# Eight weight products of a selected-token network: four of them moved from the rounds of a selection into the making of a list

## The chip, the cores and the metric

The kernel runs on one core of one Trainium2 chip. The metric is the device time in microseconds (us) of one execution. The median of three runs of the kernel before is 1208.15 us (1207.38 to 1210.46). A change smaller than 0.3% of that, 3.6 us, is called no change in this document.

## The reference, cut to what matters

The whole computation is a graph network, a linear-attention mix and, last, a feed-forward network on about half of the nodes. Only the last part is touched:

```python
# _L0_ffn_ref, x: (1, 6250, 256), the layer-normed output of what comes before
weights = (einsum('bsd,do->bso', x, wr) + br)[..., 0]      # one weight a node
_, idx = top_k(weights, k)                                 # k = 3125
sel_idx = idx[:, :kk]                                      # kk = 3124 nodes
sel = take_along_axis(x, sel_idx[:, :, None], axis=1)
h = gelu(einsum('bkd,dh->bkh', sel, w1) + b1)              # 256 -> 1024
y = einsum('bkh,hd->bkd', h, w2) + b2                      # 1024 -> 256
y = y * weights of the selected nodes
out = zeros.at[sel_idx].set(y) + x
```

## The kernel before

The five engines run five separate programs, each in the order in which its code is written. They wait for each other through semaphores. That written order is what sets the order of the work here; there is no scheduler.

Nodes are handled in tiles of 128, and four tiles make a group. The node stage (13 groups) ends near 994 us of the trace. From there the kernel does this:

- **The rounds of the selection.** The threshold of the top 3124 weights is found digit by digit: nine counts. In each, VectorE compares (L1256), counts (L1258) and raises `s_c`; TensorE sums the counts over the partitions with one small matmul into `psN` (L2087) and raises `s_n`; VectorE reads the sums. After the last round come two matmuls on `marks` (L2092, L2093), some VectorE work, and two transposes (L2096, L2097).
- **The blocks of the list.** The 3124 indices are made in `LBLOCKS` = 7 blocks of 512. For block b, VectorE makes `step_` ("reached", L1309); TensorE multiplies it ("ranks", L2105, into `psR` or `psC` in turn); VectorE compares into `below` ("ranked", L1316); TensorE counts with eight matmuls of one column ("places", L2112 and L2113, into `psI`, which is `psKx[1]`); VectorE writes the indices ("listed", L1320). TensorE issues `ranks(b + 1)` ahead of `places(b)`. GpSimd gathers the chosen rows `yg` by the list (L464). After the places of blocks 2, 3, 4 and 5 TensorE also transposes tile 0, 1, 2 and 3 of the first group of chosen rows (L2125, into `psT`). ScalarE copies each to `yT_hi` (`y_high`, L1751), and VectorE makes `yT_lo` (`y_low`, L1303). `y_low` of tile t stands in VectorE's program behind "ranked" of block t + 3 and ahead of "reached" of block t + 5.
- **The last network.** For each group of chosen rows the first layer (`hidden`, by L56 to L58, into `psG` = `psQ + psKx`), Gelu on ScalarE (L1763), and the second layer (L65 to L68).

All float32 weights are split into a high part (rounded to the fast matmul type) and a low part. The low part is the raw weight minus the high part, and TensorE computes it: `low_product(i)` is one float32 matmul by the identity (L2081) and one by minus the identity on the high part (L2082), each 128x512. ScalarE copies each product out of PSUM (L1738, in `last_weights`). There are eight: 0 to 3 are for the first weights `F1`, 4 to 7 for the second weights `F2w`. They go into the four PSUM banks `psW` = `psQ + psKx` in turn. One more matmul (L2094, into `psC`) spreads the bias `f2r`, and ScalarE copies it to `f2b` (L1740). `s_fp` counts these nine products, `s_fl` their copies.

ScalarE's program is `last_weights()` and then `last_network()`. So the eight copies, the copy of `f2b` and the activation of L1741, ahead of which the Gelu table is loaded, all stand ahead of `y_high` of the first tile:

```python
for i in range(8):
    act.wait_ge(s_fp, i + 1)
    ...copy the low part i (L1738)
act.wait_ge(s_fp, 9)
...copy f2b (L1740); Gelu on one column (L1741)
# last_network():
y_high(0)
```

Of the kernel before, what the change touches and what calls it, by code (L numbers as in the profile page):

```python
# [13 lines left out]
NODES, NF = 6250, 256  # L14
# [56 lines left out]
def build(nc, x, dstp, edges, u, W1, b1, W2, b2, Wqkv, bqkv, Wout, bout, wr, br, w1, fb1, w2, fb2, out):  # L71
# [10 lines left out]
    with keep:  # L82
        ksb = lambda n, s, d=f32: keep.enter_context(nc.sbuf_tensor(n, s, d))
        ident = ksb("ident", [P, P])
        ones = ksb("ones", [P, P])
# [30 lines left out]
        with ExitStack() as ctx:  # L116
# [73 lines left out]
            minus = sb("minus", [P, P], f32r)  # L190
# [209 lines left out]
            s_fh = sem("c_fh")  # L400
# [37 lines left out]

            raw_v = edges.rearrange("(q i) f -> q (i f)", i=4)
            psW = psQ + psKx  # L440
            psA, psH, psO = psT, psQ + psKx, [psR, psC]
            psN, psP, psL, psI = psT[0], psT[1], [psR, psC], psKx[1]
            psY, psG, psF = psT, psQ + psKx, [psR, psC]
# [932 lines left out]
            def _(act):  # L1376
# [349 lines left out]
                def last_weights():  # L1726
                    act.wait_ge(s_o, TILES)
                    act.wait_ge(s_fw[0], 16)
                    nc.scalar.copy(F1[0][:, :, :], rF1[:, :, :]).then_inc(s_fh, 1)
                    act.wait_ge(s_fw[1], 48)  # L1730
                    nc.scalar.copy(F2w[:, :, 0, :], rF2[:, :, :]).then_inc(s_fh, 1)
                    act.wait_ge(s_iota, 2)
                    nc.scalar.copy(rf[:, :], ri[:, :]).then_inc(s_fh, 1)
                    for i in range(8):

                        act.wait_ge(s_fp, i + 1)
                        o = psW[i % 4][:, :]
                        nc.scalar.copy(low_piece(i)[1], o if i < 4 else o.rearrange("p (m n) -> p m n", n=NF)).then_inc(s_fl, 1)  # L1738
                    act.wait_ge(s_fp, 9)
                    nc.scalar.copy(f2b[:, :], psC[:, 0:NF]).then_inc(s_fl, 1)  # L1740
                    nc.scalar.activation(gf[0][:, 0:1], ones[:, 0:1], ACT.Gelu_apprx_tanh)  # L1741

                def last_network():
# [34 lines left out]
            def _(pe):  # L1778
# [292 lines left out]
                    turn(12)  # L2071
                node_stage()

                def selection():
                    def low_product(i):

                        hi, _, raw = low_piece(i)
                        pe.wait_ge(s_fh, i // 4 + 1)
                        if i >= 4:
                            pe.wait_ge(s_fl, i - 3)  # L2080
                        nc.tensor.matmul(psW[i % 4][:, :], ident[:, :], raw, start=True, stop=False)  # L2081
                        nc.tensor.matmul(psW[i % 4][:, :], minus[:, :], hi, start=False, stop=True).then_inc(s_fp, 1)  # L2082

                    for i in range(ROUNDS + 2):

                        pe.wait_ge(s_c, i + 1)
                        nc.tensor.matmul(psN[:, 0:DIG], ones_b[:, :], cnt[:, :], start=True, stop=True).then_inc(s_n, 1)  # L2087
                        if i >= 1:
                            low_product(i - 1)
                    pe.wait_ge(s_c, ROUNDS + 3)  # L2090
                    flat = marks[:, :, :].rearrange("p h t -> p (h t)")
                    nc.tensor.matmul(psP[:, 0:2 * TILES], ones_b[:, :], flat, start=True, stop=True)  # L2092
                    nc.tensor.matmul(psP[:, P:P + 2 * TILES], tri_b[:, :], flat, start=True, stop=True).then_inc(s_n, 1)  # L2093
                    nc.tensor.matmul(psC[:, 0:NF], ones[0:1, :], f2r[0:1, :], start=True, stop=True).then_inc(s_fp, 1)  # L2094
                    pe.wait_ge(s_c, ROUNDS + 4)
                    nc.tensor.transpose(psP[0:TILES, 2 * P:3 * P], diff[:, :], ident[:, :])  # L2096
                    nc.tensor.transpose(psP[0:TILES, 3 * P:4 * P], cumsel[:, :], ident[:, :]).then_inc(s_n, 1)  # L2097
                    pe.wait_ge(s_fl, 9)

                def ranks(b):  # L2100

# [14 lines left out]
                def last_network():  # L2116
# [12 lines left out]
                    def hidden(g, m):  # L2129
                        nt, rows = chosen(g)  # L2130
                        n = slice(0, nt * rows)
                        if m == 0:
                            pe.wait_ge(s_yl, g * GT + nt)
                        if g * KH + m >= 4:
                            pe.wait_ge(s_ge, g * KH + m - 3)
                        if g == 0 and m == 3:
                            pe.wait_ge(s_lst, LBLOCKS)
                        for c in range(KF):
                            ins = split3(nc, psG[m % 4][:, n], [f[:, c, m * P:(m + 1) * P] for f in F1], [y[:, c, n] for y in yT],
                                         c == 0, c == KF - 1)  # L2140
                        ins.then_inc(s_u1, 1)
                    ranks(0)
                    for b in range(LBLOCKS):
                        if b + 1 < LBLOCKS:
                            ranks(b + 1)
                        if b == LBLOCKS - 1:
                            for m in range(2):
                                hidden(0, m)
                        places(b)
                        transposes(0, FIRST.get(b, ()))  # L2150
                    for g in range(SGROUPS + 1):
                        nt, rows = chosen(g)
# [48 lines left out]
```

## Time and profile before

| what | us |
|---|---|
| median of three runs | 1208.15 |
| lowest and highest run | 1207.38, 1210.46 |
| the profiled execution | 1211.47 |
| its span | 1209.7 |
| TensorE (PE) busy | 1033.7 (85% of the span) |
| VectorE (DVE) busy | 1011.3 (84%) |
| ScalarE (ACT) busy | 485.1 (40%) |
| GpSimd (POOL) busy | 464.5 (38%) |

The profile describes one execution. Its span is the time from the first to the last recorded instruction, and 1.8 us of the execution lie around it. PEld is TensorE's weight load, which overlaps its matmuls. PEclk is the granted TensorE clock as a share of 2.4 GHz: 0.50 is 1.2 GHz, 1.00 is 2.4 GHz. A busy share over the whole span says little about one stage, so the stretches around the selection are read by themselves below.

### The profile page before, as it was taken

The page shows a single profiled execution, that of the slowest core. Times are in us where ns is not written, and L with a number is a line of the kernel's source. Part 1 is how long each engine was busy: PE and PEld are TensorE (multiplying, and loading weights), DVE is VectorE, ACT ScalarE, POOL GpSimd, SP SyncE. Part 2 cuts the span into 40 slices and gives each one's busy share as a digit, 9 for nine tenths or more (in the row PEclk, how much of TensorE's full clock was granted, in tenths as well). Part 3 has the DMA queues.
Part 4 walks back from the last instruction along what each step waited for, and adds up shares of the span by engine and source line. Part 5 has one row for each costly group of instructions (what it writes and reads, how often), then busy time and mean ns, then how long its engine had stood idle before and what let it go on. Part 6 is the DMA issues. An engine that isn't in the chain of part 4 may idle for free.

```text
span 1209.7 us, 15753 instructions
## 1 busy us (share of the span) xinstructions
PE 1033.7 (85%) x4561; PEld 769.1 (64%) x4561; DVE 1011.3 (84%) x2405; ACT 485.1 (40%) x1439; POOL 464.5 (38%) x344
## 2 busy tenths in 40 slices
PE   3287799999978384379999999999999986899996
PEld 1154456656545362157888888888888872588885
DVE  6899999999999999858898888988888557575672
ACT  3556577778842152022332233332233323233430
POOL 0088830888200002376466444565441000223411
PEclk9698899999996787589999999999999966699997
DMA  9899999999988999433344433343331130111100
GB/s 314 307 318 370 343 353 363 354 367 365 337 320 325 407 414 343 188 98 103 97 153 130 130 123 102 125 152 123 127 111 46 46 100 13 37 36 48 53 26 20
DMA packets 96013, 235.53 MB, mean 195 GB/s; under 512 B 13703, under 2 KB 68764, under 8 KB 89682
## 3 DMA queue, kind: packets, MB, share of 16 engines
q1 hardware_dynamic: 49890, 156.61, 34.9%
q10 hardware_dynamic: 31248, 44.71, 10.3%
q0 software_dynamic: 14816, 33.53, 10.1%
q8 instruction: 24, 0.39, 0.1%
q14 instruction: 35, 0.29, 0.1%
HBM read 154.25 MB, written 80.55 MB: 194 GB/s over the span
## 4 chain that ended last, share of the span: by engine, by line
PE 53%; DVE 4%; issue 1%; ACT 0%; DMA 0%; POOL 0%; DVEq 0%; POOLq 0%
PE psR L67 5%; PE psQ L56 5%; PE psQ L57 5%; PE psQ L58 5%; PE psKx L56 5%; PE psKx L57 5%; PE psKx L58 5%; PE psC L67 5%; PE psR L68 3%; PE psC L68 2%; PE psT L2012 1%; PE psQ L2033 1%; PE psKx L2033 1%; PE psR L66 1%; PE psC L66 1%
## 5 line engine op out<-in xcount | busy, mean ns | idle before, releaser
L459 POOL DMA_INDIRECT graw<-in_edge_attr,ic x98 | 143.2, 1461 | 74.9 <-DVE ob L949 39.4
L946 DVE SCALAR_TENSOR_TENSOR ob<-ob,mQ,mx 128x96 f32<-128x96 f32 x392 | 122.3, 312 | 4.4
L949 DVE SCALAR_TENSOR_TENSOR ob<-ob,kQ,xb 128x96 f32<-128x96 f32 x392 | 122.0, 311 | 0.1
L636 POOL DMA_INDIRECT near<-ends_d,blki x49 | 87.8, 1791 | 72.9 <-DVEq L854 58.3
L636 POOL DMA_INDIRECT near<-in_dst,rowi x49 | 87.8, 1793 | 59.7 <-DVEq L863 45.1
L1688 ACT ACTIVATE hT_hi<-psQ 128x512 fp32r<-128x512 f32 (+1 forms) x52 | 29.8, 574 | 185.6 <-PE psQ L2033 185.6
L1829 PE MATMUL psQ<-Wqk,xT 128*128 128x512 f32 (+1 forms) x196 | 96.6, 617 | 0.0
L934 DVE TENSOR_TENSOR xb<-xb 128x1536 f32<-128x1536 f32 x49 | 86.1, 1758 | 1.7
L932 DVE TENSOR_TENSOR mx<-xb 128x1536 f32<-128x1536 f32 x49 | 85.6, 1747 | 1.1
L1688 ACT ACTIVATE hT_hi<-psKx 128x512 fp32r<-128x512 f32 (+1 forms) x52 | 29.8, 574 | 96.1 <-PE psKx L2033 96.1
L67 PE MATMUL psR<-W2w,hT_hi 128*128 128x512 f32 (+1 forms) x175 | 66.3, 414 | 1.7 <-DVE x L1101 1.7
L729 POOL DMA_INDIRECT out_x<-zo,lst x25 | 24.5, 979 | 109.8 <-DVE zo L1368 109.8
L464 POOL DMA_INDIRECT yg<-yrow_d,lst x25 | 25.0, 1001 | 96.6 <-DVE lst L1320 89.3
L67 PE MATMUL psC<-W2w,hT_hi 128*128 128x512 f32 x168 | 60.9, 399 | 0.0
L484 POOL DMA_INDIRECT grow<-scan_d,ic x49 | 53.4, 1089 | 16.2 <-issue 14.6
L1829 PEld LDWEIGHTS psQ<-Wqk,xT 128*128 128x128 f32 (+1 forms) x196 | 39.4, 201 | 28.1 <-issue 25.4
L1850 PE MATMUL psKx<-xn,kc 128*128 128x257 f32 (+1 forms) x196 | 51.4, 385 | 4.2 <-ACT kc L1490 4.2
L1091 DVE SCALAR_TENSOR_TENSOR hT_lo<-psQ,hT_hi 128x512 fp32r<-128x512 f32 (+1 forms) x52 | 33.9, 653 | 23.4 <-ACT hT_hi L1688 23.4
L684 POOL COPY ic<-idx 128x12 int32 (+2 forms) x11 | 2.1, 194 | 132.6 <-PE psC L66 132.6
L1841 PE MATMUL psC<-WvoI,xT 128*128 128x256 f32 (+1 forms) x196 | 52.0, 389 | 0.0
L68 PE MATMUL psR<-W2w,hT_lo 128*128 128x256 f32 (+1 forms) x175 | 50.3, 287 | 0.0
L650 POOL COPY ic<-idx 128x12 int32<-128x12 int32 x2 | 1.9, 956 | 121.6 <-DVEq L895 121.6
(499 smaller groups left out, 3270.0 us busy)
## 6 DMA issues: line engine op xcount, KB each, us to landing
xb<-in_edge_attr SPq DMA_DIRECT2D x49, 1536.0 KB, 10.6
scan_d<-ob SPq DMA_DIRECT2D x49, 768.0 KB, 6.3
yrow_d<-yr SPq DMA_DIRECT2D x48, 132.0 KB
xg<-in_x ACTq DMA_DIRECT2D x12, 512.0 KB, 10.3
xT_d<-xT ACTq DMA_DIRECT2D x12, 512.0 KB, 7.2
base_d<-dcur ACTq DMA_DIRECT2D x12, 512.0 KB
qT_d<-qT ACTq DMA_DIRECT2D x12, 512.0 KB, 8.8
out_x<-xres SPq DMA_DIRECT2D x48, 128.0 KB
```

The lines of the kernel that those rows point to most:

```text
L56: nc.tensor.matmul(out, lh, rh, start=start, stop=False)
L57: nc.tensor.matmul(out, lh, rl, start=False, stop=False)
L58: return nc.tensor.matmul(out, ll, rh, start=False, stop=stop)
L67: nc.tensor.matmul(out, lh, both.rearrange("p h n -> p (h n)"), start=start, stop=False)
L68: return nc.tensor.matmul(out[:, 0:NF], ll, both[:, 0, :], start=False, stop=False)
L459: nc.gpsimd.indirect_dma_start(out=to.rearrange("p i f -> p (i f)"), out_offset=None, in_=raw_v, in_offset=bass.IndirectOffsetOnAxis(ap=ic ...
L636: nc.gpsimd.indirect_dma_start(out=near[:, t, :], out_offset=None, in_=table, in_offset=bass.IndirectOffsetOnAxis(ap=rows[:, t:t + 1], axi ...
L932: nc.vector.tensor_tensor(mx[:, :, :, :], xp[:, :, :, 0, :], xp[:, :, :, 1, :], ALU.max).then_inc(s_tree, 1)
L934: nc.vector.tensor_tensor(xp[:, :, :, 0, :], xp[:, :, :, 0, :], xp[:, :, :, 1, :], ALU.add).then_inc(s_tree, 1)
L946: nc.vector.scalar_tensor_tensor(o[:, q, 0:EF], prev[:, 0:EF], mQ[:, bass.ds(c * TQ + q, 1)], mx[:, q, 0, :], ALU.min, ALU.max).then_inc(s ...
L949: nc.vector.scalar_tensor_tensor(o[:, q, EF:AGG], prev[:, EF:AGG], kQ[:, bass.ds(c * TQ + q, 1)], X[:, q, 0, :], ALU.mult, ALU.add).then_i ...
L1829: ins = nc.tensor.matmul(o, xT[:, c, t * P:t * P + rows], Wqk[:, c, :], start=False, stop=(c == KF - 1))
```

## The change

The products 4 to 7 leave the rounds of the selection. `low_product(4 + b)` now stands right behind `places(b)` for b = 0 to 3. The products use three banks (`psV`, which leaves out `psKx[1]`, the bank of the places) in place of four. The bias matmul moves from behind the `marks` matmuls into the round i = 5, and ScalarE copies `f2b` as its fifth copy in place of its ninth. The first hidden product now waits for all nine copies. `selection` ends with a wait for five copies in place of nine.

```diff
+            psV = psQ + psKx[0:1]
@@ ScalarE, last_weights
                     for i in range(8):
-                        act.wait_ge(s_fp, i + 1)
-                        o = psW[i % 4][:, :]
+                        act.wait_ge(s_fp, i + 1 if i < 4 else i + 2)
+                        o = psV[i % 3][:, :]
                         nc.scalar.copy(low_piece(i)[1], ...).then_inc(s_fl, 1)
-                    act.wait_ge(s_fp, 9)
-                    nc.scalar.copy(f2b[:, :], psC[:, 0:NF]).then_inc(s_fl, 1)
+                        if i == 3:
+                            act.wait_ge(s_fp, 5)
+                            nc.scalar.copy(f2b[:, :], psC[:, 0:NF]).then_inc(s_fl, 1)
                     nc.scalar.activation(gf[0][:, 0:1], ones[:, 0:1], ACT.Gelu_apprx_tanh)
@@ TensorE, low_product (now outside selection)
-                        if i >= 4:
-                            pe.wait_ge(s_fl, i - 3)
+                    if i >= 3:
+                        pe.wait_ge(s_fl, i - 2 if i < 7 else i - 1)
@@ TensorE, selection
                         nc.tensor.matmul(psN[:, 0:DIG], ones_b[:, :], cnt[:, :], start=True, stop=True).then_inc(s_n, 1)
-                        if i >= 1:
+                        if 1 <= i < 5:
                             low_product(i - 1)
+                        if i == 5:
+                            pe.wait_ge(s_fh, 2)
+                            nc.tensor.matmul(psC[:, 0:NF], ones[0:1, :], f2r[0:1, :], start=True, stop=True).then_inc(s_fp, 1)
...
-                    nc.tensor.matmul(psC[:, 0:NF], ones[0:1, :], f2r[0:1, :], start=True, stop=True).then_inc(s_fp, 1)
...
-                    pe.wait_ge(s_fl, 9)
+                    pe.wait_ge(s_fl, 5)
@@ TensorE, hidden
+                        if g == 0 and m == 0:
+                            pe.wait_ge(s_fl, 9)
@@ TensorE, the loop over the blocks
                         places(b)
+                        if b < 4:
+                            low_product(4 + b)
                         transposes(0, FIRST.get(b, ()))
```

On TensorE, the end of the selection before. L2081 and L2082 are a low product, L2087 the sum of a count, L2092 and L2093 the `marks` matmuls, L2094 the bias, L2105 the ranks:

```order
L2087 MATMUL psT<-cnt,ones_b 128x15 [waits c_c]
L2081 MATMUL psKx<-rF_181,ident 128x512 [waits c_fl,c_fh]
L2082 MATMUL psKx<-F2w,minus 128x512
L2092 MATMUL psT<-marks,ones_b 128x98 [waits c_c]
L2093 MATMUL psT<-marks,tri_b 128x98
L2094 MATMUL psC<-f2r,ones 128x256
L2096 MATMUL psT<-ident,diff 49x128 [waits c_c]
```

The same place of the kernel changed (there L2094 is the bias and L2089 a count, of which the last three follow each other; L2097, L2098 and L2100 are what L2092, L2093 and L2096 were):

```order
L2094 MATMUL psC<-f2r,ones 128x256 [waits c_fh]
L2089 MATMUL psT<-cnt,ones_b 128x15 [waits c_c] x3
L2097 MATMUL psT<-marks,ones_b 128x98 [waits c_c]
L2098 MATMUL psT<-marks,tri_b 128x98
L2100 MATMUL psT<-ident,diff 49x128 [waits c_c]
```

The low product and the bias matmul that stood around the `marks` matmuls are gone from there.

On TensorE, from the last places of block 2 to the ranks of block 5 in the kernel changed. L2082 and L2083 are now a low product, L2129 the transposes of a tile of chosen rows, L2109 the ranks, L2116 and L2117 the places:

```order
L2117 MATMUL psKx<-rows__236,step__196 128x1
L2082 MATMUL psQ<-rF_181,ident 128x512 [waits c_fl,c_fh]
L2083 MATMUL psQ<-F2w,minus 128x512
L2129 MATMUL psT<-ident,yg_199 128x128 [waits d_g00]
L2129 MATMUL psT<-ident,yg_199 128x128
L2109 MATMUL psR<-step__196,rows__236 128x512 [waits c_cmp,c_step]
...
L2082 MATMUL psQ<-rF_181,ident 128x512 [waits c_fl,c_fh]
L2083 MATMUL psQ<-F2w,minus 128x512
L2129 MATMUL psT<-ident,yg_199 128x128 [waits d_g01]
L2129 MATMUL psT<-ident,yg_199 128x128
L2109 MATMUL psC<-step__196,rows__236 128x512 [waits c_cmp,c_step]
```

A product has come in ahead of each pair of transposes, and ahead of the ranks; before, the transposes stood right behind the places. The eight places of block 3 stand where the line of dots is.

On ScalarE, the order of its copies in the kernel changed, around the same place:

```order
L1742 COPY f2b<-psC 128x256 [waits c_fp]
L1739 CAST F2w<-psQ 128x2x256 [waits c_fp]
L1739 CAST F2w<-psKx 128x2x256 [waits c_fp]
L1739 CAST F2w<-psQ 128x2x256 [waits c_fp] x2
L1743 ACT_TABLE_LOAD
L1743 ACTIVATE gf_190<-ones 128x1
L1753 CAST yT_hi<-psT 128x2x128 [waits d_y] x4
```

The four copies of the second weights, the table load and the activation stand ahead of the four copies to `yT_hi`, as before; the copy of `f2b` stands ahead of them now.

## Rows read from the trace of the kernel before

**Rows 1.** Busy time by engine in four stretches (length, busy us and instructions, PEclk).

```profile
1007.00:1014.00 7.00, 3.32 (x10) 1.02 (x8) 5.95 (x14) 1.76 (x3) 0.00 (x0) 0.99 0.00 0
1014.00:1027.00 13.00, 10.88 (x19) 4.29 (x20) 9.76 (x27) 2.31 (x4) 0.00 (x0) 0.50 0.00 0
1027.00:1051.00 24.00, 18.31 (x79) 10.70 (x78) 12.92 (x36) 4.55 (x10) 7.78 (x8) 0.50 0.17 46
1051.00:1190.00 139.00, 139.00 (x726) 117.50 (x724) 92.13 (x192) 51.29 (x94) 40.40 (x41) 1.00 0.12 39
```

**Rows 2.** Waits from 1030 to 1056 us (total, times, longest).

```profile
ACT yT_hi L1751 <- PE psT L2125: 14.3, 4, 9.1
PEld psKx L2112 <- DVE below L1316: 3.7, 5, 1.0
PE psT L2125 <- DMA yg<-yrow_d,lst: 0.3, 1, 0.3
```

**Rows 3.** Timeline, last round (start us, duration us, engine, line; in brackets idle before).

```profile
1022.80 0.92 DVE L1258 TENSOR_REDUCE cnt<-reach 128x15 bf16<-128x735 f32 x1
...
1023.84 0.20 PE L2087 MATMUL psT<-cnt,ones_b 128*128 128x15 bf16 x1 [0.53 <-DVEq L1259]
...
1023.94 2.04 PE L2081 MATMUL psKx<-rF,ident 128*128 128x512 f32 x2
...
1025.24 0.27 DVE L1275 SCALAR_TENSOR_TENSOR marks<-wgt,thr,valid 128x49 bf16<-128x49 f32 x1
...
1026.21 0.30 PE L2092 MATMUL psT<-marks,ones_b 128*128 128x98 bf16 x1
```

**Rows 4.** Timeline, a low product and its copy, at either clock.

```profile
1008.41 1.10 PE L2081 MATMUL psKx<-rF,ident 128*128 128x512 f32 x2
...
1009.78 0.59 ACT L1738 CAST F_lo<-psKx 128x512 fp32r<-128x512 f32 x1 [1.59 <-PE psKx L2082]
...
1020.84 2.04 PE L2081 MATMUL psKx<-rF,ident 128*128 128x512 f32 x2
...
1023.34 0.59 ACT L1738 CAST F2w<-psKx 128x512 fp32r<-128x512 f32 x1 [2.51 <-PE psKx L2082]
```

**Rows 5.** Timeline, ScalarE at the end of the copies.

```profile
1027.78 0.37 ACT L1740 COPY f2b<-psC 128x256 f32<-128x256 f32 x1 [0.75 <-PE psC L2094]
...
1028.17 1.28 ACT L1741 ACT_TABLE_LOAD   x1
...
1029.46 0.20 ACT L1741 ACTIVATE gf<-ones 128x1 f32<-128x1 f32 x1
```

**Rows 6.** Timeline, TensorE: first places of block 0, ranks, first places of block 1.

```profile
1033.10 0.19 PE L2112 MATMUL psKx<-ones_b,below 128*128 128x1 bf16 x1 [0.36 <-DVE below L1316]
...
1033.97 0.58 PE L2105 MATMUL psR<-step__196,rows__236 49*128 49x512 bf16 x1
...
1034.96 0.19 PE L2112 MATMUL psKx<-ones_b,below 128*128 128x1 bf16 x1 [0.41 <-DVE below L1316]
```

**Rows 7.** Timeline, blocks 3 and 4, with the first chosen tile.

```profile
1038.81 0.37 ACT L1751 CAST yT_hi<-psT 128x256 fp32r<-128x256 f32 x1 [9.14 <-PE psT L2125]
...
1039.22 0.42 DVE L1303 TENSOR_TENSOR yT_lo<-psT,yT_hi 128x256 fp32r<-128x256 f32 x1 [0.58 <-ACT yT_hi L1751]
...
1039.24 0.19 PE L2112 MATMUL psKx<-ones_b,below 128*128 128x1 bf16 x1
...
1040.18 0.69 PE L2125 MATMUL psT<-ident,yg 128*128 128x128 f32 x2
...
1040.37 0.69 DVE L1316 SCALAR_TENSOR_TENSOR below<-psR,rf 128x512 bf16<-128x512 f32 x1
...
1040.80 0.60 PE L2105 MATMUL psC<-step__196,rows__236 49*128 49x512 bf16 x1
...
1041.34 0.19 PE L2112 MATMUL psKx<-ones_b,below 128*128 128x1 bf16 x1
```

**Rows 8.** Timeline, the first hidden product.

```profile
1045.98 0.79 PE L56 MATMUL psQ<-yT_hi,F_hi 128*128 128x512 f32 x1 [0.92 <-DVE yT_lo L1303]
```

More of the change, by code:

```diff
@@ L2072, in _, with low_product @@
                 node_stage()
-                def selection():
-                    def low_product(i):
-                        hi, _, raw = low_piece(i)
-                        pe.wait_ge(s_fh, i // 4 + 1)
-                        if i >= 4:
-                            pe.wait_ge(s_fl, i - 3)
-                        nc.tensor.matmul(psW[i % 4][:, :], ident[:, :], raw, start=True, stop=False)
-                        nc.tensor.matmul(psW[i % 4][:, :], minus[:, :], hi, start=False, stop=True).then_inc(s_fp, 1)
+                def low_product(i):
+                    hi, _, raw = low_piece(i)
+                    pe.wait_ge(s_fh, i // 4 + 1)
+                    if i >= 3:
+                        pe.wait_ge(s_fl, i - 2 if i < 7 else i - 1)
+                    nc.tensor.matmul(psV[i % 3][:, :], ident[:, :], raw, start=True, stop=False)
+                    nc.tensor.matmul(psV[i % 3][:, :], minus[:, :], hi, start=False, stop=True).then_inc(s_fp, 1)
+                def selection():
                     for i in range(ROUNDS + 2):
```

## The prediction

> **What bounds the kernel now.** I read the busy shares first; they name TensorE and VectorE and decide nothing. Then I read the stretches around the change [rows 1]. From 1051 to 1190 us TensorE is busy in all of the 139 us at a granted clock of 1.00: nothing later can absorb a delay of the first hidden product, and nothing there can be early unless that product is. From 1014 to 1051 us the granted clock is 0.50 (1.2 GHz) and TensorE has idle time. There the question is what it waits for. In the rounds it waits for VectorE's counts: the count ends at 1022.80 + 0.92 = 1023.72 and TensorE answers at 1023.84, after 0.12 us [rows 3]. The low product behind it (1023.94) lies in time in which VectorE is making the next count, so in an ordinary round it costs nothing. In the blocks of the list TensorE and VectorE answer each other: TensorE waits for "below" five times, 3.7 us by the weight loads [rows 2]. ScalarE is idle; its longest wait there is 9.1 us, for the first transposed tile. So the cover of a product in the rounds is VectorE's time, and the cover that the list offers has to be measured in the same way: the gap between TensorE being free and its next input being there.
>
> **What a product costs on TensorE.** At 1.2 GHz the last one begins at 1023.94, and the marks matmul queued behind it begins at 1026.21: 2.27 us. Its copy on ScalarE can begin 1023.34 - 1020.84 = 2.50 us after it begins [rows 3, 4]. At 2.4 GHz that second figure is 1009.78 - 1008.41 = 1.37 us, 1.13 less, so I estimate 2.27 - 1.13 = 1.14 us of TensorE for a product at full clock.
>
> **What goes from the rounds.** Products 4 to 7 leave four rounds. Three of them were hidden: worth nothing. The last was not. "marks" was ready at 1025.24 + 0.27 = 1025.51, so with the same answer of 0.12 us the marks matmul could have begun at 1025.63; it began at 1026.21 [rows 3]. That gives back 0.58 us, since all that follows hangs on it. What is late next is VectorE's own chain to the transposes. The bias matmul and its copy move to a round in which a product would have stood; they take less than that product, and stay hidden.
>
> **What comes into the list.** I keep the clock of the trace of before, at 1.2 GHz, and move the start of each part (times from here on are us after 1000). Places begin at 33.10 in block 0, and the next instruction starts 0.87 later, at 33.97 [rows 6]. Before, that is the ranks matmul, and the places of block 1 begin at 34.96: 0.99 us in which TensorE has only the ranks to do. The ranks take 41.34 - 40.80 = 0.54, the transposes of one tile 40.80 - 40.18 = 0.62 [rows 7]. So the idle time in a block is 0.99 - 0.54 = 0.45 us, and 2.27 us are put there.
>
> Block by block: product 4 from 33.97 to 36.24, ranks to 36.78, places of block 1 at 36.78 (before 34.96, so 1.82 later). Then 0.87, product 5 from 37.65 to 39.92, ranks, places of block 2 at 40.46. Product 6 from 41.33 to 43.60, transposes of tile 0 to 44.22, ranks, places of block 3 at 44.76 (before 39.24, so 5.52 later). The 0.3 us in which the first transposes waited for the gather [rows 2] are gone in this, as the rows have landed long before. Product 7 begins at 44.76 + 0.87 = 45.63.
>
> **The wait that takes over.** ScalarE's copies are in written order: `y_high` of tile 0 stands behind the copy of product 7, the Gelu table load and its activation. Before, all of that was over at 1029.66 [rows 5], nine us ahead of its first tile. Now: the copy of product 7 begins at 45.63 + 2.50 = 48.13 and takes 0.59 [rows 4]; 0.02 later the load, 29.46 - 28.17 = 1.29 from its start to the activation, 0.20 for that [rows 5]. `y_high` of tile 0 begins at 50.23, though its transposes were there since 44.2. Queued behind it is VectorE: `y_low` of tile 0 stands in its program ahead of "reached" of block 5 and "ranked" of block 4, without which TensorE has no places of block 4. From before: `y_low` begins 39.22 - 38.81 = 0.41 after `y_high`, "ranked" begins 40.37 - 39.22 = 1.15 later, takes 0.69 [rows 7], and 0.12 to TensorE. Places of block 4 at 50.23 + 0.41 + 1.15 + 0.69 + 0.12 = 52.60, where they were at 41.34: 11.26 later. TensorE's own work would have allowed 49.06 (product 7 ends at 47.90, transposes to 48.52, ranks to 49.06), so 3.54 of it is ScalarE's table load and copies in VectorE's way.
>
> From the places of block 4 to the first hidden product nothing is added; it took 45.98 - 41.34 = 4.64 us [rows 7, 8] and takes the same. The new wait of that product for nine copies is met by then. GpSimd gets blocks 1 to 3 of the list later, but its gathers for the second group are wanted only a whole group later. Sum: 11.26 - 0.58 = 10.7 us. The profiled execution then takes 1211.47 + 10.7 = 1222.2 us; it lies 3.3 above the median of the runs, so on the median the forecast is 1208.15 + 10.7 = 1218.8 us.
>
> What the trace doesn't show is the clock in a list stage that contains products. Upper bound: it stays at 1.2 GHz and rises some 1 to 1.5 us later in the first layer than before (it took 5 us there, 1045.98 to about 1051 [rows 1, 8]), 1220.5. Lower bound: full clock for all of it, worked out below, 1210.5. I take the nearest rows. From 1014 to 1027 us there were products in every round of 3.1 us, TensorE was busy for 10.88 of 13 us, and the clock stayed at 0.50 throughout [rows 1]. In the changed list there is one in every 3.7 us.
>
> **Rivals.**
>
> *The clock rises on the way.* For: it stood at 0.99 from 1007 to 1014 [rows 1] with no more than one product a round, and TensorE now works without a gap from 1033 to 1048. Against: the 13 us named above. Price: product 7 at full clock brings its copy 1.13 earlier, product 6 the same, and a first layer that begins at full clock saves half of its 5.3 slow us, 2.65. All three give 4.9, one gives 1.1: 1213.9 to 1217.7 us, middle 1216.
>
> *The clock is full from the first moved product until the last network; not slower.* This is where the change would break even. Products of 1.14, ranks of 0.27 (half), transposes of 0.31, places as before: places of block 1 at 35.38, of block 2 at 37.66, of block 3 at 40.25; product 7 at 41.12, its copy at 42.49, `y_high` at 44.59, places of block 4 at 46.96. That is 5.62 late; less 0.58 and 2.65 it is 2.4 us, 1210.5 us, no change by the bound below. It decides from product 4 on: if that one takes 2.27 us it is out. Against it speaks further that TensorE would be idle for some 3 us behind the transposes of tile 1, and before, with idle time in the rounds, the clock fell at 1014.
> The Trainium skill ("TensorE: Matmul & The Clock Gate", What's actually happening) says that the throttled state is the default and that activity releases it. Taken alone that rule speaks for this rival, since the change fills gaps; by it the result would be 1210.5, by the 13 busy and slow us of rows 1 it is 1218.8.
>
> *ScalarE's order does not bite.* If the copies to `yT_hi` did not wait behind the table load, only TensorE's sum is left: 49.06 - 41.34 - 0.58 = 7.1 us, 1215.3. For: 9 us of slack before [rows 2]. Against: the order of ScalarE's instructions, which stands as it was, and the slack was there only because the products were over at 1026.
> The same page of the Trainium skill (the section on the 16 sub-arrays) says that ScalarE's and VectorE's queues are strictly first in, first out, with which this rival would be excluded; no row of before tests it.
>
> **How the numbers follow.** The forecast 0.70, with its own range from 1217.5 to 1220.5. The clock on the way 0.20. Full clock 0.05. ScalarE's order without effect 0.03. The last 0.02 is for something slower than 1220.5. The range 1214.0 to 1220.5 takes in the forecast and most of the first rival. About 0.3%, or 3.6 us, is what a measurement of this kernel can tell from no change. Only the full clock lies inside it, and the lowest end of the first rival comes near: faster 0.01, same 0.06, slower 0.93.
>
> **What would show it.** In the changed profile: no product in the rounds 5 to 8 and the marks matmul about 0.1 us behind "marks"; places starts of blocks 0 to 3 about 3.7, 3.7 and 4.3 us apart, with idle time of TensorE near nothing; the table load at about 1048 us; VectorE idle for some 8 us ahead of the first `yT_lo`, released by ScalarE; TensorE idle ahead of the ranks of block 5 for about 3 us; first hidden product near 1056.7 us; from there on the same 139 us at full clock. The forecast is wrong if the copies of product 5 to 7 come 1.4 us behind their products in place of 2.5 (then the clock rose), if VectorE's wait is short, or if TensorE shows idle time between product 4 and the places of block 1.

## The result, and the profile after

The median of seven runs of the kernel changed is 1219.15 us (1216.78 to 1225.23). Seven runs of the kernel before, among them the three shown above, have a median of 1210.46 us (1207.1 to 1217.69). The ratio is 1.0076 with a 95% interval of 1.0043 to 1.0109: slower by about 9 us (5.2 to 13.2). The profiled execution has a span of 1220.8 us, 11.1 us above that of before.

The stretches of TensorE that answer to [rows 1], of the kernel changed (length, busy us and instructions by engine, then the granted clock):

```profile
1014.00:1027.00 13.00, 2.31 (x8) 0.91 (x6) 10.86 (x27) 0.96 (x2) 0.00 (x0) 0.55 0.00 0
1027.00:1046.00 19.00, 14.02 (x44) 6.32 (x44) 8.30 (x26) 1.76 (x3) 7.83 (x8) 0.50 0.19 50
1046.00:1053.00 7.00, 3.64 (x22) 2.29 (x21) 2.20 (x6) 2.61 (x5) 0.00 (x0) 0.98 0.08 21
1053.00:1063.00 10.00, 9.08 (x31) 6.17 (x31) 2.90 (x8) 2.57 (x6) 0.00 (x0) 0.50 0.00 0
1063.00:1202.00 139.00, 139.00 (x730) 117.79 (x728) 92.36 (x195) 51.13 (x96) 40.72 (x41) 1.00 0.12 39
```

TensorE has left the rounds (2.31 us busy where it was 10.88), and the last network is what it was, 139 us without a gap at full clock, only later. New is a stretch at full clock from 1046 to 1053, inside the making of the list; it is lost again before the first layer.

Of the waits from 1030 to 1056 us of the kernel changed, these bear on the change (those of before are in [rows 2]):

```profile
ACT F2w L1739 <- PE psQ L2083: 25.4, 3, 19.7
DVE yT_lo L1304 <- ACT yT_hi L1753: 7.3, 2, 7.1
...
PEld psC L2109 <- DVE step__196 L1310: 3.5, 2, 3.3
```

ScalarE now waits for products in place of the first tile, VectorE waits 7.1 us for ScalarE's first `yT_hi`, and TensorE, which had only short waits there before, waits 3.3 us by its weight load, 3.1 us by its matmul, for VectorE's `step_` of block 5.

The same order of events as in [rows 3, 4, 6 and 7], in the timeline of the kernel changed (L2089 is the count, L2097 the marks, L2116 the places, L2082 a product, L2109 the ranks, L1739 ScalarE's copy of a product):

```profile
1001.46 0.20 PE L2089 MATMUL psT<-cnt,ones_b 128*128 128x15 bf16 x1 [6.21 <-DVEq L1246]
...
1025.36 0.19 PE L2089 MATMUL psT<-cnt,ones_b 128*128 128x15 bf16 x1 [2.91 <-DVEq L1260]
...
1026.76 0.27 DVE L1276 SCALAR_TENSOR_TENSOR marks<-wgt,thr,valid 128x49 bf16<-128x49 f32 x1
...
1027.15 0.26 PE L2097 MATMUL psT<-marks,ones_b 128*128 128x98 bf16 x1 [1.59 <-DVEq L1277]
...
1034.00 0.18 PE L2116 MATMUL psKx<-ones_b,below 128*128 128x1 bf16 x1 [0.36 <-DVE below L1317]
...
1034.93 2.08 PE L2082 MATMUL psQ<-rF,ident 128*128 128x512 f32 x2
...
1037.36 0.60 PE L2109 MATMUL psR<-step__196,rows__236 49*128 49x512 bf16 x1
...
1037.90 0.19 PE L2116 MATMUL psKx<-ones_b,below 128*128 128x1 bf16 x1
...
1046.92 1.13 PE L2082 MATMUL psQ<-rF,ident 128*128 128x512 f32 x2
...
1048.31 0.59 ACT L1739 CAST F2w<-psQ 128x512 fp32r<-128x512 f32 x1 [2.44 <-PE psQ L2083]
1048.91 1.28 ACT L1743 ACT_TABLE_LOAD   x1
...
1050.31 0.63 ACT L1753 CAST yT_hi<-psT 128x256 fp32r<-128x256 f32 x2
1050.70 0.42 DVE L1304 TENSOR_TENSOR yT_lo<-psT,yT_hi 128x256 fp32r<-128x256 f32 x1 [7.08 <-ACT yT_hi L1753]
...
1051.57 0.39 PE L2109 MATMUL psC<-step__196,rows__236 49*128 49x512 bf16 x1 [3.08 <-DVE step__196 L1310]
...
1052.24 0.18 PE L2116 MATMUL psKx<-ones_b,below 128*128 128x1 bf16 x1 [0.28 <-DVE below L1317]
...
1056.83 0.79 PE L56 MATMUL psQ<-yT_hi,F_hi 128*128 128x512 f32 x1 [0.92 <-DVE yT_lo L1304]
```

Where the 11.1 us of the span are: the first count of the selection already begins 1.52 us later than the 999.94 us of before, ahead of anything changed. That is the spread between executions. From the last count to the first hidden product it took 1045.98 - 1023.84 = 22.14 us before [rows 3, 8] and 1056.83 - 1025.36 = 31.47 us now: 9.33 us. From the first hidden product to the end it took 163.72 and 163.97 us: 0.25 us, since the clock rises about half a microsecond later in the first layer. 1.52 + 9.33 + 0.25 = 11.1.

So the experiments are compared by this **stage time**, last count to first hidden product. It leaves out the spread of the 1000 us ahead of it: the whole runs of the kernel before lie between 1207.1 and 1217.69 us. It also leaves out the last network, so where the clock of the first layer changes, the text says so. One trace is one execution: two kernels below were profiled twice, and their stage times differ by 1.53 and 2.13 us. A smaller difference between two kernels counts here only where the rows show the step that it comes from.

All ratios are of undisturbed runs; one run of ten without products in the list took 1729.67 us, at a granted clock of 0.557 in place of 0.91, and is left out.

### The profile page after: what moved, and what is told of

Read it like the earlier page. It is cut to its first block, busy times and chain, and to the rows that moved or that the text cites. A ratio compares the mean times of both kernels' runs of the same rounds, so it can differ in the third digit from the quotient of the medians.

```text
span 1220.8 us, 15755 instructions
## 1 busy us (share of the span) xinstructions
PE 1026.5 (84%) x4561; PEld 765.9 (63%) x4561; DVE 1008.2 (83%) x2405; ACT 485.0 (40%) x1439; POOL 464.3 (38%) x344
## 4 chain that ended last, share of the span: by engine, by line
PE 53%; DVE 4%; ACT 1%; issue 0%; POOL 0%; DVEq 0%
PE psR L67 5%; PE psQ L56 5%; PE psQ L57 5%; PE psQ L58 5%; PE psKx L56 5%; PE psKx L57 5%; PE psKx L58 5%; PE psC L67 5%; PE psR L68 3%; PE psC L68 2%; PE psT L2014 1%; PE psQ L2035 1%; PE psKx L2035 1%; PE psR L66 1%; PE psC L66 1%; DVE reach L1257 1%
## 5 line engine op out<-in xcount | busy, mean ns | idle before, releaser
L1831 PEld LDWEIGHTS psQ<-Wqk,xT 128*128 128x128 f32 (+1 forms) x196 | 39.3, 200 | 28.1 <-issue 25.5
```

The lines of the kernel that those rows point to most:

```text
L1831: ins = nc.tensor.matmul(o, xT[:, c, t * P:t * P + rows], Wqk[:, c, :], start=False, stop=(c == KF - 1))
```

## The experiments

Ratios are to the kernel before on the same chip, with the 95% interval. The four of the experiments without a ratio have one execution each.

| kernel | stage time, us | expected | ratio |
|---|---|---|---|
| before | 22.14 | | |
| changed | 31.47 | 32.8 (22.14 + 10.7) | 1.0076 [1.0043, 1.0109] |
| table load early | 31.32 | 30.0 | 1.0052 [1.0032, 1.0072] |
| the same again | 29.79 | 31.3 or 30.0 | |
| copies in order | 27.71 | 28.2 | 1.0024 [1.0008, 1.0041] |
| product 7 behind marks | 21.31 | 21.56 | 0.9986 [0.9974, 0.9998] |
| no products in the list | 21.47 | 21.6 | 0.9973 [0.9959, 0.9988] |
| products twice | 33.04 | 35 to 40.6 | 1.0102 [1.0060, 1.0144] |
| rounds filled | 31.96 | 32.1 | 1.0106 [1.0059, 1.0153] |
| product 7 alone moved | 25.37 | 23.0 | 1.0016 [0.9996, 1.0036] |
| the same again | 23.24 | 23.2 or 25.4 | |
| products half as wide | 28.34 | 28.1 | 1.0049 [1.0026, 1.0072] |
| twice, table load early | 32.20 | 31.5 | |
| twice, copies in order | 29.60 | 29.9 or less | |

### No products in the list

```diff
@@ ScalarE
-                    for i in range(8):
+                    for i in range(4):
...
+                    nc.scalar.copy(F2w[:, :, 1, :], F2w[:, :, 0, :].bitcast(f32)).then_inc(s_fl, 4)
@@ TensorE
-                        if b < 4:
-                            low_product(4 + b)
```

> The kernel changed, with the products 4 to 7 and their copies left out: the low parts of the second weights are filled by one plain copy of the high parts early, so the output is not the reference's; only the time counts. My theory (the whole delay comes from the products in the list, by TensorE's time and ScalarE's order): stage time as before less the 0.58 us that the empty last round gives back, 21.6 us, total 0.6 us less than before. Rival (something else of the change costs, as the bank order, the moved bias, the wait of the first hidden product): stage time clearly above 22.1 us. Rival (the clock falls further without products and that costs): first hidden products slow for longer than the 5.3 us of before.

Timeline of this kernel, the last count and the first hidden product:

```profile
1023.50 0.20 PE L2090 MATMUL psT<-cnt,ones_b 128*128 128x15 bf16 x1 [2.90 <-DVEq L1260]
...
1044.97 0.79 PE L56 MATMUL psQ<-yT_hi,F_hi 128*128 128x512 f32 x1 [0.92 <-DVE yT_lo L1304]
```

21.47 us, as expected: the other edits of the change (three banks, the moved bias, the new waits) cost nothing that can be seen in this stage, and the whole delay comes with the four products and their copies. The ratio, 0.9973, is 3.3 us below the kernel before (1.7 to 5.0), more than the 0.67 us of the stage time; the rows of this stage do not show where the rest comes from.

### The Gelu table load ahead of the copies

```diff
                             nc.scalar.copy(f2b[:, :], psC[:, 0:NF]).then_inc(s_fl, 1)
+                            nc.scalar.activation(gf[0][:, 0:1], ones[:, 0:1], ACT.Gelu_apprx_tanh)
-                    nc.scalar.activation(gf[0][:, 0:1], ones[:, 0:1], ACT.Gelu_apprx_tanh)
```

> The kernel changed, with ScalarE's Gelu table load and its activation placed right behind the copy of f2b, ahead of the copies of the products 4 to 7. The measure is the stage time: from the last count matmul of the selection to the first hidden product. It was 1045.98 - 1023.84 = 22.14 us before and 1056.83 - 1025.36 = 31.47 us in the kernel changed. My theory (VectorE, and behind it TensorE, wait for the first copy to yT_hi, which stands in ScalarE's order behind the copy of product 7 and the table load): the copy to yT_hi comes 1.29 + 0.20 = 1.49 us earlier and so does everything behind it, stage time 30.0 us, VectorE's wait ahead of yT_lo 5.6 us in place of 7.08. Rival (only TensorE's own work counts, ScalarE is not in the way): stage time unchanged, 31.5 us. The clock may add or take about 1 us in either.

Timeline of this kernel:

```profile
1019.59 0.20 PE L2089 MATMUL psT<-cnt,ones_b 128*128 128x15 bf16 x1 [2.90 <-DVEq L1260]
...
1041.31 2.08 PE L2082 MATMUL psQ<-rF,ident 128*128 128x512 f32 x2
...
1043.85 0.58 ACT L1739 CAST F2w<-psQ 128x512 fp32r<-128x512 f32 x1 [3.75 <-PE psQ L2083]
1044.33 0.66 ACT L1753 CAST yT_hi<-psT 128x256 fp32r<-128x256 f32 x2
...
1050.91 0.79 PE L56 MATMUL psQ<-yT_hi,F_hi 128*128 128x512 f32 x1 [0.92 <-DVE yT_lo L1304]
```

The stage time missed its number: 31.32, near the rival's. But the step that was cut did what it should: from the start of the copy of product 7 to the first `yT_hi` it is now 0.48 us, where it was 50.31 - 48.31 = 2.00. The most of what ate it was the clock: product 7 took 43.85 - 41.31 = 2.54 us to its copy, where it took 1.39 in the kernel changed. One trace does not settle it; a second one does.

> The kernel changed with the early table load, profiled once more, for the clock. If the clock of product 7 is a matter of the execution and the table load is worth 1.5 us, the stage time is 31.3 us with product 7 at 1.2 GHz (2.5 us from its start to its copy) or about 30.0 us with it at 2.4 GHz (1.4 us). A third value, or 31.5 with product 7 at 2.4 GHz, would speak against the theory.

```profile
1025.18 0.19 PE L2089 MATMUL psT<-cnt,ones_b 128*128 128x15 bf16 x1 [2.91 <-DVEq L1260]
...
1046.84 1.12 PE L2082 MATMUL psQ<-rF,ident 128*128 128x512 f32 x2
...
1048.23 0.58 ACT L1739 CAST F2w<-psQ 128x512 fp32r<-128x512 f32 x1 [2.54 <-PE psQ L2083]
...
1049.99 0.39 PE L2109 MATMUL psC<-step__196,rows__236 49*128 49x512 bf16 x1 [1.58 <-DVE step__196 L1310]
...
1054.97 0.79 PE L56 MATMUL psQ<-yT_hi,F_hi 128*128 128x512 f32 x1 [0.92 <-DVE yT_lo L1304]
```

Product 7 at full clock, stage time 29.79, VectorE's wait ahead of the first `yT_lo` 5.68 us (expected 5.6, before the edit 7.08), and TensorE's wait ahead of the ranks of block 5 is 1.58 in place of 3.08. The table load is worth 1.5 us; the clock of product 7 differs from execution to execution of one and the same kernel.

### The copy to yT_hi of tile 0 ahead of the copy of product 7

```diff
                         nc.scalar.copy(low_piece(i)[1], ...).then_inc(s_fl, 1)
+                        if i >= 6:
+                            t = i - 6
+                            act.wait_ge(s_yt, t + 1)
+                            nc.scalar.copy(yT[0][:, :, t * P:(t + 1) * P], ...psY[t % 2]...).then_inc(s_yh, 1)
                         if i == 3:
...
+                            nc.scalar.activation(gf[0][:, 0:1], ones[:, 0:1], ACT.Gelu_apprx_tanh)
-                    nc.scalar.activation(gf[0][:, 0:1], ones[:, 0:1], ACT.Gelu_apprx_tanh)
...
-                    y_high(0)
+                    y_high(0, range(2, GT))
```

> As the run with the early table load, and on ScalarE the copies to yT_hi of tile 0 and 1 stand ahead of the copies of product 6 and 7, the order in which it can have both early. My theory: VectorE no longer waits for ScalarE behind product 7, and what is left is TensorE's own work in the blocks. The ranks of block 5 then follow the transposes of tile 1 at once, so the 3.1 us of TensorE's wait there go: stage time about 31.47 - 3.3 = 28.2 us if product 7 runs at full clock as in the kernel changed, 29.3 us if not. Rival (the delay is all of it order on ScalarE): stage time near 22.1 us. Rival (TensorE alone counted already): 31.5 us. One thing may go wrong with my placing: the copy to yT_hi of tile 0 stands ahead of the copy of product 6, though product 6 is ready first; nothing but the first hidden product waits for that copy.

The text above has the order otherwise than the kernel. The copy to `yT_hi` of tile 0 stands behind the copy of product 6 and ahead of that of product 7, and the copy of tile 1 stands behind that of product 7, as the rows of ScalarE (L1739 and L1743) show. The wait in question hangs on tile 0 alone, so the test still holds.

```profile
1025.31 0.20 PE L2094 MATMUL psT<-cnt,ones_b 128*128 128x15 bf16 x1 [2.90 <-DVEq L1260]
...
1045.24 0.59 ACT L1739 CAST F2w<-psQ 128x512 fp32r<-128x512 f32 x1 [3.32 <-PE psQ L2088]
1045.72 0.38 ACT L1743 CAST yT_hi<-psT 128x256 fp32r<-128x256 f32 x1
...
1048.36 0.58 ACT L1739 CAST F2w<-psQ 128x512 fp32r<-128x512 f32 x1 [2.26 <-PE psQ L2088]
1048.85 0.38 ACT L1743 CAST yT_hi<-psT 128x256 fp32r<-128x256 f32 x1
...
1048.16 0.38 PE L2134 MATMUL psT<-ident,yg 128*128 128x128 f32 x2
1048.48 0.39 PE L2114 MATMUL psC<-step__196,rows__236 49*128 49x512 bf16 x1
...
1053.02 0.80 PE L56 MATMUL psQ<-yT_hi,F_hi 128*128 128x512 f32 x1 [0.92 <-DVE yT_lo L1304]
```

The ranks of block 5 (here L2114) follow the transposes of tile 1 (L2134) after 0.32 us, without a wait. 31.47 - 27.71 = 3.76 us of the delay came with ScalarE's order (the table load among it); 27.71 - 21.47 = 6.24 us are left, and they are TensorE's own time for the products. Of the 3.76 us, 3.39 are there at the places of block 4 (1048.80, so 23.49 us behind the last count, where it was 52.24 - 25.36 = 26.88). The other 0.37 came behind them, where the clock was still full in this trace. The rival by which ScalarE's order does not bite is out, and so is the one by which all of the delay is its order.

The total shows more than the stage time: 1.0024 is 2.9 us above the kernel before (1.0 to 5.0), while the stage time is 5.57 us above it. From the first hidden product to the end it took 161.28 us here and 163.97 us in the kernel changed. In this trace the clock was low for 3.4 us of the first layer (to about 1056.4) in place of 6.1 us; that gave 1.2 to 1.4 us. The rest of the 2.7 us lies in the last group of chosen rows.

### The last round relieved, and nothing else

```diff
-                        if i >= 1:
+                        if 1 <= i <= 7:
                             low_product(i - 1)
...                      the marks matmuls
-                    the bias matmul
+                    low_product(7)
...                      the two transposes
+                    the bias matmul
...
+                    if b == 1:
+                        pe.wait_ge(s_fl, 9)
```

The wait for the nine copies moves with them, from the end of `selection` to the ranks of block 1.

> The kernel before, with one product moved: product 7 stands behind the marks matmuls of the selection in place of ahead of them, and the bias matmul behind the two transposes. There TensorE waits for VectorE's chain of some 3 us. My theory: the marks matmul begins 0.12 us behind marks in place of 0.70, product 7 (2.27 us) and the bias are hidden, stage time 22.14 - 0.58 = 21.56 us, total time 0.6 us less than before, too little to be told by the time alone. Rival (the 0.58 us were no queueing, VectorE or the semaphore was late): stage time 22.1 us. Rival (product 7 delays the transposes): stage time above 22.1.

```profile
1022.09 0.20 PE L2087 MATMUL psT<-cnt,ones_b 128*128 128x15 bf16 x1 [0.53 <-DVEq L1259]
...
1023.87 0.26 PE L2092 MATMUL psT<-marks,ones_b 128*128 128x98 bf16 x1 [1.59 <-DVEq L1276]
1024.01 2.04 PE L2081 MATMUL psKx<-rF,ident 128*128 128x512 f32 x2
...
1027.45 0.45 PE L2096 MATMUL psT<-ident,diff 128*49 128x128 f32 x1 [0.97 <-DVEq L1292]
...
1043.40 0.79 PE L56 MATMUL psQ<-yT_hi,F_hi 128*128 128x512 f32 x1 [0.92 <-DVE yT_lo L1303]
```

From the last count to the marks it is 1.78 us where it was 26.21 - 23.84 = 2.37 [rows 3]: 0.59 us were queueing. The other 0.24 us of the gain in stage time lie behind the marks and are not assigned. Product 7 stands behind the marks, and TensorE still waits 0.97 us for VectorE after it: it is hidden. The stage time of 21.31 is the lowest of all, and the whole kernel is the only version with all of its computation that is faster than the one before, by 0.14% (0.02 to 0.26%); that is less than the 0.3% set above as what can be told from no change, so the trace carries this claim more than the time.

### The rounds filled again, the list as changed

```diff
+                        if i >= 6:
+                            pe.wait_ge(s_fl, 5)
+                            ...the two matmuls of product i - 1 into psV[i % 3], read by nobody
```

> The kernel changed, with the products of the rounds kept as well: TensorE computes a product in the rounds 6, 7 and 8 whose result nobody reads, and the list is as in the kernel changed. It undoes one half of the change. My theory: only the last round matters, the marks matmul is late by some 0.6 us again and the rest stays, so stage time 31.47 + 0.6 = 32.1 us (33.2 if product 7 of the list falls at 1.2 GHz this time). Rival (empty rounds let the clock fall and so made the list slow): stage time clearly less than 31, products in the list at 1.4 us to their copy.

```profile
1026.00 0.19 PE L2089 MATMUL psT<-cnt,ones_b 128*128 128x15 bf16 x1 [0.57 <-DVEq L1260]
...
1028.33 0.30 PE L2102 MATMUL psT<-marks,ones_b 128*128 128x98 bf16 x1
...
1057.96 0.79 PE L56 MATMUL psQ<-yT_hi,F_hi 128*128 128x512 f32 x1 [0.92 <-DVE yT_lo L1304]
```

31.96 us, 0.49 more than the kernel changed, and the marks are 2.33 us behind the count again. Emptying the rounds gave back half a microsecond and did not make the list slow: the two halves of the change are separate.

### Product 7 alone in the list

```diff
-                        if b < 4:
-                            low_product(4 + b)
+                        if b == 0:
+                            low_product(7)
```

with the products 4 to 6 in the rounds and the bias behind the marks, as before.

> Products 4 to 6 stay in the rounds as before, product 7 alone moves behind the places of block 0, the bias matmul stays behind the marks matmuls. My theory: 0.58 us gained in the last round; the places of block 1 1.82 us later, of which some 0.4 us are absorbed ahead of the first transposes by the wait for the gather; ScalarE has its copy and table load over about when the first tile comes. Stage time 22.14 - 0.58 + 1.43 = 23.0 us. Rival (a product costs its full 2.27 us wherever it stands in the list): 23.8 us. Rival (one product is covered by the gaps of the list): 21.5 us.

The stage time was 25.37 us, 2.4 above what was expected. The timeline shows one stretch that no theory had:

```profile
1042.32 0.16 DVE L1321 CAST lst<-psKx 128x4 int32<-128x4 f32 x1 [2.37 <-remote]
1042.36 0.37 ACT L1753 CAST yT_hi<-psT 128x256 fp32r<-128x256 f32 x1 [3.50 <-remote]
```

VectorE and ScalarE both stand still and start again within 0.04 us of each other, released by nothing that the profile can name ("remote"). The next transposes are 4.22 us behind the ones before (1039.86 to 1044.08), where the pattern is 2.09: 2.13 us.

> The kernel with product 7 alone in the list, profiled once more. The first time its stage time was 25.37 us where 23.0 was expected, and 2.1 us of it lay in one stretch in which ScalarE and VectorE both stood still ahead of the third copy to yT_hi, though the transposes were done. If that stretch belongs to this one execution and not to the place of the product, the stage time is now 23.2 us. If the moved product causes it, 25.4 us again.

```profile
1023.51 0.20 PE L2089 MATMUL psT<-cnt,ones_b 128*128 128x15 bf16 x1 [0.53 <-DVEq L1260]
...
1046.75 0.79 PE L56 MATMUL psQ<-yT_hi,F_hi 128*128 128x512 f32 x1 [0.92 <-DVE yT_lo L1304]
```

23.24 us: the stall was not there in this execution, so the place of the product does not bring it each time. What it was stays open. One product in the list costs 23.24 - 21.47 = 1.77 us: the gaps of the list hide a part of its time on TensorE (2.27 us or more), not all of it.

### Products half as wide

```diff
+                    if i >= 4:
+                        hi, raw, o = hi[:, 0, :], raw[:, 0, :], o[:, 0:NF]
```

> The kernel changed, with the products in the list half as wide (256 columns in place of 512); the other half of those low parts is left as a copy of the high part, so the output is not the reference's. My theory: a product takes 1.14 us of TensorE at 1.2 GHz and 0.45 us of each block are idle, so a block is 0.69 us longer in place of 1.82, and ScalarE's copy, table load and activation follow product 7 as before. Stage time 28.1 us, of which about 2 us are VectorE's and TensorE's wait for ScalarE. Rival (cost proportional to width alone: half of the 10.0 us between 31.47 and 21.47): 26.5 us.

```profile
1045.02 0.60 PE L2113 MATMUL psC<-step__196,rows__236 49*128 49x512 bf16 x1 [2.66 <-DVE step__196 L1310]
```

28.34 us (1021.98 to 1050.32), and TensorE's wait ahead of the ranks of block 5 is 2.66 us where about 2 were expected. Half of the width takes away 31.47 - 28.34 = 3.13 of the 10.0 us, not half of them. Two things stay: the wait of 2.66 us for ScalarE's chain, and more than half of TensorE's time. From the start of a half-wide product to the ranks behind it, it was 1.37 us (1031.55 to 1032.92), not the 1.14 expected, where a whole one took 2.43. This trace is at 1.2 GHz from 1014 us up to the first layer, while product 7 of the kernel changed ran at full clock, so at one and the same clock the saving would be larger, by an estimated 1.1 us (2.50 - 1.39).

### Products twice in the list

```diff
+                    if i >= 4:
+                        ...the two matmuls once more ahead
```

> The kernel changed, with each of the four products in the list computed twice on TensorE (the second writes the same bank again). Stage time (last count matmul to first hidden product) was 31.47 us in the kernel changed, 21.47 us without products in the list. Theory of TensorE's time: each product more costs the whole of its 2.27 us at 1.2 GHz or 1.14 at 2.4 GHz, since the idle time of a block is already used up: 31.47 + 4 x 2.27 = 40.6 us if the clock stays low, down to about 35 us if the clock rises early now that TensorE has wide matmuls for most of the time. Rival (ScalarE's order is what costs, TensorE has room): under 33 us.

```profile
1029.43 2.08 PE L2083 MATMUL psQ<-rF,ident 128*128 128x512 f32 x2
...
1033.61 0.39 PE L2112 MATMUL psR<-step__196,rows__236 49*128 49x512 bf16 x1
...
1037.17 0.39 PE L2112 MATMUL psC<-step__196,rows__236 49*128 49x512 bf16 x1
```

This number was wrong. Four more products cost 33.04 - 31.47 = 1.57 us, not 3.5 to 9. The clock rose in the first block, and from there a block with two products took 37.17 - 33.61 = 3.56 us, less than one with a single product at 1.2 GHz (3.90). The rival's bound (under 33) was missed by a hair for the same reason; it did not tell the theories apart. With the clock raised this early, ScalarE's order could be tested again.

> The products in the list twice, with the Gelu table load ahead of the copies of the products 4 to 7. With the products once, the early table load took 1.5 us off ScalarE's path and yet only 0.15 us off the stage time (31.32 against 31.47), since product 7 ran at 1.2 GHz in that trace and at 2.4 GHz in the kernel changed. With doubled products the clock rose early (stage time 33.04 us), so the clock should be the same with and without the early table load. Theory (the table load stands in VectorE's way): 33.04 - 1.5 = 31.5 us. Rival (the early table load gains nothing by itself): 33.0 us.

32.20 us, 0.84 less. TensorE's wait ahead of the ranks of block 5 is 1.58 us here, 3.08 in the kernel with doubled products alone: the 1.5 us again. The rest went to the clock, which rose during the second copy of product 4 in both, but later here, so that from the start of product 4 to the ranks behind it, it was 38.86 - 34.31 = 4.55 in place of 4.18 us, and the first layer came 0.24 us later behind the transposes of tile 2.

> The products in the list twice, with the early table load and with the copies to yT_hi of tile 0 and 1 ahead of those of product 6 and 7. Theory: TensorE's wait of 3.1 us ahead of the ranks of block 5 goes, and the clock stays high further into the list: 33.04 - 3.1 = 29.9 us or less. That would be less than the kernel changed takes with its products once (31.47 us). Rival (TensorE bound, nothing to gain): 33.0 us.

29.60 us (1021.84 to 1051.44), with eight products in the list 1.9 us less than the kernel changed takes with four. It is not the extra products that help: with the same order on ScalarE and the products once it took 27.71 us. The order is the one described there, with tile 0 behind the copy of product 6 and tile 1 behind that of product 7.

## Why the prediction was right

**Forecast and range.** 1218.8 us forecast, 1219.15 measured, inside the range. That the two are only 0.35 us apart is luck: the median of before has moved from 1208.15 to 1210.46 with more runs, and that covers a forecast delay that was too large. The comparison that counts is 10.7 us forecast against 9.33 + 0.25 = 9.6 us in the trace and about 9 us by the ratio. The interval of the ratio, 5.2 to 13.2 us, holds the forecast (10.7), the first rival's upper end (9.6) and the one without ScalarE's order (7.1), so the time alone decides between none of them; the traces do.

**The last round.** Forecast 0.58 us; the marks came 1.79 us behind the last count in place of 2.37. Right, and shown alone by the kernel with product 7 behind the marks.

**TensorE's time in the list.** The places of blocks 0 to 3 were forecast 3.68, 3.68 and 4.30 us apart; they came at 34.00, 37.90, 41.81 and 46.05, so 3.90, 3.91 and 4.24. From the start of a product to the ranks behind it, it was 37.36 - 34.93 = 2.43, not 2.27, and the places 0.93, not 0.87. Together 0.4 us too little.

**ScalarE's order.** The wait that took over was the one named: VectorE behind the first `yT_hi`, TensorE behind `step_` of block 5, 7.1 and 3.1 us. Forecast share 3.54 us at the places of block 4; with the copies in order it was 3.39 there, and 3.76 in the whole stage. From the start of `y_high` to the places of block 4 I had 2.37 us; it was 52.24 - 50.31 = 1.93, the most of it since "reached" held VectorE 0.39 us (51.04 to 51.43) in place of 0.73 (39.56 to 40.29 before).

**The clock.** This is the term that was mis-sized, and one of the prediction's own signs of being wrong appeared for one product of the three named. I kept 1.2 GHz through the list; product 7 ran at 2.4 GHz and its copy came 1.39 us behind its start, not 2.50: 1.11 us too much in the sum. The copies of products 5 and 6 came 2.54 us behind their starts, near the 2.50 forecast. So the smallest form of the first rival happened in this trace (one product, 1.1 us, 1217.7 us by its price), and in three of the other traces with four moved products (copies in order, rounds filled, the second of the early table load), but not in the first of the early table load, nor with the products half as wide. Its larger part, a first layer at full clock (2.65 us), did not come: the clock is 0.50 again from 1053 to 1063, after TensorE's wait of 3.1 us. That the wait brought it down is not shown. With the copies in order TensorE was busy for 5.79 us between 1046 and 1053, without that wait, and the clock fell at 1053.0 all the same. The argument from the 13 slow us in the rounds held for the products 4 to 6 and failed for product 7. From 1034 to 1046 us TensorE was busy in all of the 12 us at a granted clock of 0.50, and only then did the clock rise. Why it rose there and not in the first block stays open.

In sum: 0.39 too little, 1.11 and 0.44 too much, and 0.14 too much in small steps (0.10 from the copy of product 7 to `y_high`, 0.04 from the last count to the first places) give the 9.38 us at the places of block 4 for the 10.68 forecast. The mechanism was right; the price was 1.3 us too high.

**Full clock, not slower.** Out from product 4 on, by the point named: it took 2.54 us to its copy.

## What to carry to other kernels

A place on an engine is free only if the engine waits longer there than the work lasts: a round of the selection had 3 us of VectorE under a product, a block of the list 0.45 us. Work that is moved later on one engine takes with it everything that stands behind its result in another engine's order; here four copies and a table load that had been over 9 us early came to stand in front of the first tile, for 3.8 of 10 us of the stage. Before moving four pieces, look at which of them was late: only the last was, and putting that one behind the marks matmuls took 0.8 us off the stage time, as much as taking all four away (0.7).

## What the runs showed of the hardware

Two products in a block at 2.4 GHz took 3.56 us, one at 1.2 GHz 3.90 us. In the doubled kernels the granted clock rose within the first block of the list, in the kernel with single products only at 1046 us or, in one execution, not at all before the first layer. With the copies in order the clock fell at 1053.0 us though TensorE had been busy for 5.79 of the 7 us before, and with the products twice and the copies in order it fell near 1052.5, about 1 us into the first layer, in which TensorE was never idle. Two executions of one kernel differed by 31.32 - 29.79 = 1.53 us in this stage, the most of it by the clock of one product. And once, for 2.1 us, ScalarE and VectorE stood still together with a releaser that the profile calls remote; it did not come back.
